# Moving the scaling of the context from ScalarE to VectorE in a one-core decoder layer

## The reference

```python
x = x + attn(layernorm(x))            # one head of 128, softmax over 256 keys
x = x + xattn(layernorm(x), context)  # 16 heads of 64; q from x, k and v from context
x = x + ffn(layernorm(x))             # 31 chosen rows of each batch: 16 heads of 8, GELU, 512 wide

# xattn, per batch:
q, k, v = x @ Wq, context @ Wk, context @ Wv
sim = einsum('bhid,bhjd->bhij', q, k) * 64 ** -0.5
out = einsum('bhij,bhjd->bhid', softmax(sim), v)
return out.reshape(B, 256, 1024) @ Wo + bo
```

## Time and profile before

| | us |
|---|---|
| median of 3 runs | 2164.09 |
| the runs | 2164.33, 2164.09, 2159.62 |
| the profiled execution, its own time | 2161.14 |
| its span, first to last instruction | 2159.9 |
| PE busy | 2078.4 (96%) |
| POOL busy | 1936.6 (90%) |
| ACT busy | 1796.4 (83%) |
| DVE busy | 1723.5 (80%) |
| granted clock of TensorE | 0.997 |

### The profile page before, as it was taken

One profiled execution on the slowest core, in us unless ns is written; L12 is line 12 of the kernel. 1 busy time (PEld: TensorE's weight loads), 2 busy tenths in 40 slices (PEclk: granted clock), 3 DMA queues, 4 the chain that ended last, 5 costly groups with the idle time before them and its releaser, 6 DMA issues.

```text
span 2159.9 us, 57506 instructions
## 1 busy us (share of the span) xinstructions
PE 2078.4 (96%) x21697; PEld 1409.5 (65%) x21697; DVE 1723.5 (80%) x4158; ACT 1796.4 (83%) x3064; POOL 1936.6 (90%) x1129
## 2 busy tenths in 40 slices
PE   8999999999999999999999999999999999999998
PEld 4667666666766666666666666667666666666664
DVE  7778878787887878879687787887878788886864
ACT  5888898888888888898788888888888888888872
POOL 3899999999999899999899998998999999899991
PEclk9999999999999999999999999999999999999999
DMA  3211000010100001010010100101000010100000
GB/s 75 59 38 30 2 16 16 2 29 2 30 2 10 21 2 29 2 30 2 11 29 2 30 2 2 29 2 29 2 19 21 2 29 2 17 2 2 2 11 11
DMA packets 70483, 35.16 MB, mean 16 GB/s; under 512 B 58944, under 2 KB 68032, under 8 KB 70208
## 3 DMA queue, kind: packets, MB, share of 16 engines
q1 hardware_dynamic: 69104, 31.28, 6.2%
q10 hardware_dynamic: 1104, 0.20, 0.1%
HBM read 16.46 MB, written 2.10 MB: 9 GB/s over the span
## 4 chain that ended last, share of the span: by engine, by line
PE 73%; DVE 13%; issue 6%; ACT 5%; POOL 2%; DMA 0%; DVEq 0%; SPq 0%; ACTq 0%; POOLq 0%
PE PS L585 13%; PE PS L626 13%; PE PS L586 13%; PE PS L602 11%; PE PS L604 10%; DVE EH L1102 5%; PE PS L649 4%; PE PS L636 2%; DVE over L1128 2%; PE PS L659 2%; ACT PF L910 2%; POOL EL L1580 2%; ACT EH L917 1%; ACT over L932 1%; DVE junk L1373 1%
## 5 line engine op out<-in xcount | busy, mean ns | idle before, releaser
L1580 POOL TENSOR_TENSOR EL<-PF,EH 128x1024 f16<-128x1024 f32 x828 | 1761.7, 2154 | 132.6 <-DVE EH L1102 60.7
L910 ACT ACTIVATE PF<-PS 128x512 f32<-128x512 f32 x1664 | 973.4, 600 | 218.8 <-PE PS L586 203.2
L602 PE MATMUL PS<-Ch,EH 128*128 128x97 f16 (+1 forms) x6656 | 762.2, 207 | 35.6 <-POOL EL L1580 32.0
L602 PEld LDWEIGHTS PS<-Ch,EH 128*128 128x128 f16 (+1 forms) x6656 | 604.3, 97 | 283.2 <-issue 109.4
L1102 DVE TENSOR_SCALAR_CACHE_REDUCE EH<-PF 128x1024 f16<-128x1024 f32 x621 | 746.0, 1209 | 17.6 <-ACT PF L910 17.6
L604 PE MATMUL PS<-Cl,EL 128*128 128x97 f16 (+1 forms) x6656 | 758.9, 206 | 0.0
L1128 DVE CUSTOM_DVE_ANT_1 over<-over,PS 128x802 f32<-128x802 f32 x512 | 505.1, 987 | 289.7 <-PE PS L626 146.5
L604 PEld LDWEIGHTS PS<-Cl,EL 128*128 128x128 f16 (+1 forms) x6656 | 594.6, 98 | 155.0 <-issue 1.4
L585 PE MATMUL PS<-AH,ChT 98*128 98x512 f16 x1664 | 635.2, 382 | 8.9 <-ACT PF L910 6.2
L586 PE MATMUL PS<-AL,ClT 96*128 96x512 f16 x1664 | 632.9, 380 | 0.0
L932 ACT ACTIVATE over<-PS 128x802 f32<-128x802 f32 x512 | 431.3, 842 | 32.7 <-PE PS L626 12.3
(11 more groups left out here) (250 smaller groups left out, 1653.4 us busy)
## 6 DMA issues: line engine op xcount, KB each, us to landing
Cf<-in_ctx SPq DMA_DIRECT2D x16, 576.0 KB
X<-in_x SPq DMA_DIRECT2D x16, 128.0 KB, 2.5
out_x<-X SPq DMA_DIRECT2D x16, 128.0 KB, 1.7
msk<-in_attention_mask SPq DMA_DIRECT2D x4, 256.0 KB, 4.5
AH<-mh SPq DMA_DIRECT2D x63, 2.0 KB
xWqT<-in_xWqT SPq DMA_DIRECT2D x2, 256.0 KB, 5.9
xWo<-in_xWo SPq DMA_DIRECT2D x2, 256.0 KB, 3.8
fw<-in_fw SPq DMA_DIRECT2D x2, 256.0 KB, 3.1
```

Source lines behind the costliest of these rows:

```text
L602: pe.matmul(PS[:, 6, u0:u0 + DC + 1], EH[0:kr, r, qs], Ch[j][0:kr, t, 0:DC + 1], start=(t == 0 and q == 0), stop=False, skip_group_check=True)
L910: act.activation(PF[:, n % PRING, :], PS[0:KP, 4 + n % 2, :], ACT.Exp).then_inc(sg("ex"), 1)
L1580: pool.tensor_tensor(EL[:, r - 1:r + 1, :], PF[:, f - 1:f + 1, :], EH[:, r - 1:r + 1, :], ALU.subtract).then_inc(sg("lo_pool"), 1)
```

## The change

`ctx_scale` of batches 1 to 15 is taken out of ACT's list and put into DVE's, at the same place of the stream. It is the form that batch 0 had already: one `tensor_scalar` over 128 x 1248 f32, in place, with no `accum_out`. The semaphores stay the same ones.

```diff
-                elif k == "ctx_scale" and s.a[0] > 0:
-                    b, = s.a
-                    w.wait_ge(sg("sigma"), b + 1)
-                    act.activation(Cf[:, :, :], Cf[:, :, :], ACT.Copy,
-                                   scale=sigma[0:KP, b % 4:b % 4 + 1]).then_inc(sg("c_scaled"), 1)
...
-                elif k == "ctx_scale" and s.a[0] == 0:
-                    w.wait_ge(sg("sigma"), 1)
-                    dve.tensor_scalar(Cf[:, :, :], Cf[:, :, :], sigma[0:KP, 0:1], None,
+                elif k == "ctx_scale":
+                    b, = s.a
+                    w.wait_ge(sg("sigma"), b + 1)
+                    dve.tensor_scalar(Cf[:, :, :], Cf[:, :, :], sigma[0:KP, b % 4:b % 4 + 1], None,
                                       ALU.mult).then_inc(sg("c_scaled"), 1)
```

## The result

The changed kernel takes 2214.61 us (median of 4 runs, 2211.58 to 2215.91); the kernel before, run beside it, 2162.91 us. The ratio is 1.0246, with a 95% interval of 1.0234 to 1.0258. The change costs 51.7 us; the forecast was 2170, with a range up to 2179.

What follows compares the result with a forecast made beforehand. PE, busy 96% of the span, was taken as the bound. Stalls of 13 x 0.61 plus 0.20 in batch 2, less 1.22 gained in batch 1, gave +6.9 us: forecast 2170 us, range 2161 to 2179.

Steps and rivals of the forecast that it cites:

- the turn at POOL's end: DVE's scaling, batch 5: waits for POOL's running low part to end at 516.46, goes next, ends at 517.19.
- rival (c): Scaling loses its turn to POOL's next low part; base 2.70 us late, fourteen times, +37 us, 2200 us; chance 0.10.
- the 28 cases of L1207: Argument against a lost turn: L1207 beside busy POOL, started 0.7 to 1 us before a low part's end, always got in next.
- The 0.61 us of stall per place: PE's base waits for DVE's delayed fold, starting at 518.16 and not 517.55; 0.61 us in 13 places.
- (d): PE is held by ACT at all places, hidden in the timeline; 1.2 us back at each, 18 us, 2146 us; chance 0.05.
- (b): The stall is given back where PE waits for an exponential about 15 us later; 4.1 us return, +2.8, 2166; chance 0.13.
- (a): The scaling on DVE does not wait for POOL; no stall of the base, -1.2 us, 2163 us; chance 0.12.

Runs made afterwards that it cites:

- `lo_at_scale`: Changed kernel, batches 2 to 15: an unread operation of L1207's kind at the scaling's place, the scaling two places later with accum_out; 2209.43 us (one run).
- `sweep`: Changed kernel with a small extra DVE operation, longer from batch to batch, between round and scaling in batches 3 to 15; 2208.9 us (one run).
- `fill`: Changed kernel with 11 dummy matmuls of 512 columns on PE ahead of each base that waits; 2193.79 us, ratio 1.0166 to the kernel before.
- `one_port`: Changed kernel with the scaling in the accumulating form (accum_out that nobody reads), at the same place; 2167.18 us against 2158.71 for the kernel before, ratio 1.0048.
- `late_one_port`: Changed kernel with the scaling both given an accum_out and moved behind the next fold and reciprocal; 2159.27 us, ratio 0.9998 to the kernel before.
- `late`: Changed kernel with the plain scaling of batches 2 to 15 moved two places later, behind the fold and reciprocal; 2212.73 us, ratio 1.0248 to the kernel before.
- `early`: Changed kernel with the scaling one place earlier on DVE, ahead of the round; 2181.24 us, ratio 1.0096 to the kernel before.

## Why the prediction was wrong

**What failed: the turn at POOL's end.** The step was "I take the scaling to wait for POOL's end at 516.46 and to end 0.86 - 0.13 = 0.73 us behind it". It ended 0.66 us behind an end, but of the next low part. This was rival (c): its mechanism, in 13 of the 14 places, its duration of 3.5 (measured 3.48 to 3.50), its base 2.70 us late. From the start of what follows the round to the base there are 4.45 us now (523.54 to 527.99), against 1.83 in the earlier trace rows: 2.62 late. Its condition was also named rightly (decided at POOL's end), its chance, 0.10, was not.

**Why it was thought unlikely.** The argument against (c) was the 28 cases of L1207. They had the right kind and a like distance from POOL's end, but were taken at another place; `lo_at_scale` shows that this very operation loses at the scaling's place. The one case of the plain kind that was at hand, L1384, lost whenever POOL had a low part ready, and the prediction put this down to its starting only 0.05 us before an end. `sweep` moved the scaling from 0.66 to 0.25 us before the end, and it lost in all of batches 3 to 15; nearness to the end was not what made it lose.

**What was missing: the clock.** The largest case, (c), came to +37 us. The idle time of PE did grow by 34.1. The other 20.5 us stood in no case: of the thirteen holes of 2.45 us in a PE that is almost never idle otherwise, nine are followed by 3.4 or 6.8 us at 1.2 GHz. `fill` put work into the holes and got 17 to 20 us back. The profile before had three such stretches, 13.9 us in all, and the prediction did not ask what stands in front of them: one, of 6.8 us from 1062.1, begins at the end of a hole of 1.76 us in PE (1060.88 to 1062.63).

**The size of the forecast's own term.** The 0.61 us of stall per place is what would have come without the lost turn: `one_port`, whose scaling takes 1.50 us as the forecast's did (1.4 to 1.5), stalls bases by 0.5 us and costs 8.5 us, against a sum of 6.9. That the two durations are alike is luck: the forecast's was half waiting, that of `one_port` is all the operation's own time. In batch 2, where the turn was not lost, the base waited 0.20 us, as forecast, and the scaling took 1.23:

```profile
136.34 1.23 DVE L1170 TENSOR_SCALAR Cf<-Cf,sigma 128x1248 f32<-128x1248 f32 x1
137.48 0.98 DVE L1123 CUSTOM_DVE_ANT_1 over<-over,PS 128x802 f32<-128x802 f32 x1
```

```profile
138.53 0.52 PE L626 MATMUL PS<-ChT,AH 96*128 96x401 f16 x2 [0.20 <-DVE pmax L1123]
```

**What was right.** ACT's 20.4 us are worth nothing on the path (`late_one_port`, 0.9998), so (d) falls. Nothing is given back (b): PE's idle time grew by 34.1 us, and thirteen holes of 2.45 us are 31.9. Batch 1 gains 1.22 us at its place (1.48 to 0.26). (a) falls with the first scaling that took more than 0.86.

**The exclusion.** The page cited in the prediction, "SBUF — State Buffer" of the Trainium skill, section "SBUF: two separate sides", says that of the two engines the first to start blocks the other for a whole instruction. The scalings of the changed kernel agree: beside a running low part of POOL none ended before it, and the one that got in, in batch 2, stretched POOL's next low part to 2.71 us. The step that failed lies behind it, at the moment when the pair comes free: the prediction took the waiting instruction to be next, and POOL's next one, which became ready later, went first, in `late` two of them in a row (5.38 us).

## What to carry to other kernels

A plain `tensor_scalar` on VectorE beside a busy GpSimd should be priced at the end of GpSimd's next instruction as well as of the running one, unless GpSimd is known to have nothing ready then. Both ends were met here, and the later one is not even the worst (`late`); the form with `accum_out` costs more by itself and had none of this risk (1.50 us in all 16). Evidence that such an operation gets its turn holds for its place only, not for its kind. When a hole is opened in a TensorE that was always busy, count matmuls behind it at half speed as well: here that made a hole of 2.45 us cost 3.9 to 4.0, while no hole of 1.5 us had this effect.

## What the runs showed of the hardware

- A VectorE instruction that waits for GpSimd is not always next in line: it lost to one instruction in 13 places (3.49 us for 0.86) and to two in a row in `late` (5.36 to 5.38 us).
- Whether it got in went, at the scaling's place in batches 3 to 15, with when GpSimd's next instruction became ready: not up to 1.81 us behind the start of a running one of 2.14 us, but from 1.85. With that at 1.5 us, VectorE's asking anywhere from 1.47 to 1.88 us lost. In batch 2 five of six got in at 1.67, so this is not the whole rule.
- The end is always alike: 0.66 or 0.67 us behind the end of the GpSimd instruction, for an operation of 0.86 us alone.
- Behind 9 of the 13 holes of 2.45 us the granted clock stood at 0.5 for 3.41 or 6.83 us, behind the 14 shorter holes of `early` never. `fill`, with 7.8 us at 0.5 in place of 56.1, was 17 to 20 us faster.
